# Last attention of a Flamingo-style block: per-head context scores in row tiles, one reduction for head 0's maximum, an early load of the exponential table, the residual part of the norm moved by one tile

## What is computed

```python
xn = layer_norm(x, g_x, b_x)          # here x is the context, 77 rows for each batch
ln = layer_norm(latents, g_l, b_l)    # the 1024 tokens
q = ln @ Wq;  k, v = split(concat([xn, ln], axis=1) @ Wkv)   # 16 heads of 64; 77 + 1024 keys
sim = (q * 64 ** -0.5) @ k.T          # per head
sim = where(full_mask, sim, max_neg)  # masks the 77 context keys alone
out = concat_heads(softmax(sim) @ v) @ Wout
return layer_norm(out, g_o, b_o)      # then x = x + tanh(g) * this
```

## Time and profile before

| | |
|---|---|
| median of three runs | 2142.96 us |
| the profiled execution | 2142.78 us, span 2140.9 us |
| busy over the span: PE, weight loads, DVE, ACT, GpSimd | 91%, 62%, 69%, 46%, 35% |
| stage 6, the 128 tiles | 1108.9 to about 2022 us |

### The profile page before, as it was taken

How to read it: one execution, slowest core, us unless ns; L and a number is a source line. 1 busy time by engine, 2 the same in 40 slices (tenths; PEclk the granted TensorE clock), 3 DMA queues, 4 the chain that set the end, 5 groups by cost and what they waited for, 6 DMA issues and landing times.

```text
span 2140.9 us, 32958 instructions
## 1 busy us (share of the span) xinstructions
PE 1954.5 (91%) x11541; PEld 1319.1 (62%) x11541; DVE 1485.3 (69%) x2932; ACT 975.0 (46%) x2083; POOL 752.8 (35%) x1146
## 2 busy tenths in 40 slices
PE   6997899688799979988879999999989999998899
PEld 3884899434499967874555555555655555554554
DVE  5774111475244458877868999999779999998655
ACT  5662334343012252227855555555445555554445
POOL 1002111002312200000026777777546777777400
PEclk9897899888999999998989999999999999999999
DMA  3703799304299860002002333333213333333201
GB/s 112 203 2 111 268 327 327 113 0 145 97 298 320 284 218 1 1 8 77 1 20 71 81 81 81 81 81 81 63 42 76 78 80 82 80 77 81 51 1 39
DMA packets 191184, 226.85 MB, mean 106 GB/s; under 512 B 28939, under 2 KB 167085, under 8 KB 191021
## 3 DMA queue, kind: packets, MB, share of 16 engines
q1 hardware_dynamic: 183725, 201.98, 32.2%
q0 software_dynamic: 7296, 22.78, 3.2%
HBM read 127.64 MB, written 29.91 MB: 74 GB/s over the span
## 4 chain that ended last, share of the span: by engine, by line
PE 45%; ACT 5%; DVE 4%; issue 1%; ACTq 0%; DVEq 0%
PE ps L641 41%; ACT w_odd L1791 3%; PE ps L1206 1%; PE ps L1207 1%; PE ps L1107 1%; DVE small L2520 1%; ACT L1791 0%; DVE w_odd L2529 0%; DVE small L2404 0%; ACT arena L1780 0%; PE ps L1116 0%; ACT xn_tok L1643 0%; DVE small L2516 0%; DVE arena L2477 0%; DVE lnst L2470 0%
## 5 line engine op out<-in xcount | busy, mean ns | idle before, releaser
L1902 POOL COPY arena<-w_odd 32x512 f32<-32x512 f32 x1024 | 623.7, 609 | 293.0 <-DVE w_odd L2529 240.7
L641 PE MATMUL ps<-arena,w_odd 128*128 128x128 f32 (+4 forms) x2352 | 441.9, 443 | 3.0 <-DVE arena L2196 1.2
L641 PE MATMUL ps<-arena 128*64 128x256 f32 (+4 forms) x3248 | 392.2, 370 | 8.3 <-DVE arena L2327 4.4
L2529 DVE STREAM_TRANSPOSE w_odd<-w_odd 128x1024 f32<-128x1024 f32 x256 | 315.8, 1244 | 25.4 <-ACT w_odd L1791 17.1
L641 PEld LDWEIGHTS ps<-arena 128*64 128x64 f32 (+4 forms) x3248 | 258.3, 155 | 120.1 <-issue 22.5
L1791 ACT ACTIVATE w_odd<-ps,small 128x1101 f32<-128x1101 f32 x256 | 301.0, 1178 | 53.2 <-DVE small L2521 52.2
L641 PEld LDWEIGHTS ps<-arena,w_odd 128*128 128x128 f32 (+3 forms) x2352 | 246.8, 188 | 107.3 <-issue 102.0
L2520 DVE TENSOR_REDUCE small<-ps 128x1 f32<-128x589 f32 (+1 forms) x256 | 253.6, 991 | 16.4 <-PE ps L641 16.4
L1776 ACT ACTIVATE arena<-ps 77x256 f32<-77x256 f32 x128 | 48.6, 379 | 321.8 <-PE ps L1207 321.7
L1886 POOL DMA_INDIRECT token_rows<-arena x62 | 59.9, 965 | 306.4 <-DVE arena L2217 306.4
L641 PE MATMUL ps<-xn_feat,w_even 128*128 128x512 f32 (+1 forms) x352 | 141.2, 533 | 6.1 <-DVE xn_feat L2101 1.9
(11 more groups left out here) (397 smaller groups left out, 3016.5 us busy)
## 6 DMA issues: line engine op xcount, KB each, us to landing
arena<-w_odd SPq DMA_DIRECT2D x1024, 64.0 KB
w_odd<-in_s_w SPq DMA_DIRECT2D x32, 1024.0 KB
w_odd<-in_s_wgu SPq DMA_DIRECT2D x30, 704.0 KB
w_even<-in_s_w SPq DMA_DIRECT2D x15, 1024.0 KB
arena<-expert_rows_in SPq DMA_DIRECT2D x62, 130.0 KB
w_odd<-in_s_wd SPq DMA_DIRECT2D x30, 256.0 KB
out_feat<-in_s_wgu SPq DMA_DIRECT2D x10, 704.0 KB, 4.2
expert_rows_in<-zero_row POOLq DMA_DIRECT2D x1, 5070.0 KB, 32.9
```

Source lines behind the costliest of these rows:

```text
L641: return pe.matmul(o, lhsT, rhs, start=start, stop=stop, **kw)
L1902: pool.tensor_copy(s6_d[u % 4][32 * j:32 * j + 32, :, 256 * i:256 * i + 256], s6_pm[u % 2][32 * i:32 * i + 32, :, 256 * j:256 * j + 256]). ...
L2529: dve.transpose(s6_pm[u % 2][:, h], s6_pm[u % 2][:, h]).then_inc(t6_done, 1)
```

## The change

1. PE computes the context scores of each head as a product of its own, contracting over that head's 64 partitions and 77 columns wide. The order is: context of head 0; first tokens of head 1; first tokens of head 0; a wait of PE for the completion of the context product of head 0; context of head 1; last tokens of head 0; last tokens of head 1. There are four increments of the semaphore a tile, before there were three.
2. `s6_kx` holds the 77 columns once; the memset on GpSimd, its semaphore and one of two ACT copies go.
3. DVE starts on the context scores when both are there, and takes head 0's maximum in one reduction of 1101 columns, behind the last token product. The reduction of 512 columns and one use of the two-operand minimum go.
4. Behind each square root of the output norm ACT takes an exponential of one column into a scratch cell.
5. `added(g)` runs one tile later, in the even tile ahead of `normed(g + 1)`, for g % 32 from 28 to 30; for g % 32 = 31 it stays where it was.

```diff
-        s6_kx = [cut(WE, 8704 + 154 * i, 2, C) for i in range(2)]
+        s6_kx = [cut(WE, 8704 + 154 * i, C) for i in range(2)]
...
-                    mm(s6_both, s6_q[n % 2][:, q0:q0 + P], s6_kx[n % 2]).then_inc(a6_s, 1)
-                    for i in range(2):
-                        for h in range(2):
-                            r = 64 * h
-                            last = mm(PS[:, 3 * h + i, :], s6_q[n % 2][r:r + 64, q0:q0 + P], s6_k[n % 2][r:r + 64, i * 512:(i + 1) * 512])
-                        last.then_inc(a6_s, 1)
+                    def tokens(h, i):
+                        r = 64 * h
+                        return mm(PS[:, 3 * h + i, :], s6_q[n % 2][r:r + 64, q0:q0 + P], s6_k[n % 2][r:r + 64, i * 512:(i + 1) * 512])
+
+                    def context(h):
+                        r = 64 * h
+                        return mm(s6_both[:, h], s6_q[n % 2][r:r + 64, q0:q0 + P], s6_kx[n % 2][r:r + 64])
+
+                    context(0).then_inc(a6_s, 1)
+                    tokens(1, 0)
+                    tokens(0, 0).then_inc(a6_s, 1)
+                    pe.wait_ge(a6_s, 4 * u + 1)
+                    context(1).then_inc(a6_s, 1)
+                    tokens(0, 1)
+                    tokens(1, 1).then_inc(a6_s, 1)
...
-                        if n < 2:
-                            act.wait_ge(z6_in, 1)
-                        act.activation(s6_kx[n % 2][0:64, 0], PS[0:64, bank, 2 * P:2 * P + C], ACT.Copy)
-                        last = act.activation(s6_kx[n % 2][64:P, 1], PS[64:P, bank, 2 * P:2 * P + C], ACT.Copy)
+                        last = act.activation(s6_kx[n % 2], PS[:, bank, 2 * P:2 * P + C], ACT.Copy)
...
                         act.activation(lnsd[:, t:t + 2], lnve[:, t:t + 2], ACT.Sqrt).then_inc(o6_sd, 1)
+                        act.activation(exp_cells[:, no:no + 1], zero[:, 0:1], ACT.Exp)
...
-                    pool.memset(WE[:, 8704:9012], 0.0).then_inc(z6_in, 1)
...
-                        dve.wait_ge(a6_s, 3 * u + 1)
+                        dve.wait_ge(a6_s, 4 * u + 3)
                         link(dve.tensor_tensor(s6_both, s6_both, s6_mk[:, u // 64].unsqueeze(1).broadcast_to([P, 2, C]), ALU.add))
                         dve.tensor_reduce(s6_cm[:, u % 2, 1:2], s6_both[:, 1], AX.X, ALU.max, negate=True)
-                        dve.wait_ge(a6_s, 3 * u + 2)
-                        dve.tensor_reduce(s6_cm[:, u % 2, 0:1], psf[:, 0:512], AX.X, ALU.max, negate=True)
-                        dve.wait_ge(a6_s, 3 * u + 3)
-                        for h in range(2):
-                            m = s6_nm[:, u % 2, h:h + 1]
-                            link(dve.tensor_reduce(m, s6_rest[h], AX.X, ALU.max, negate=True))
-                            dve.tensor_tensor(m, m, s6_cm[:, u % 2, h:h + 1], ALU.min).then_inc(a6_mx, 1)
+                        dve.wait_ge(a6_s, 4 * u + 4)
+                        dve.tensor_reduce(s6_nm[:, u % 2, 0:1], s6_sc[0], AX.X, ALU.max, negate=True).then_inc(a6_mx, 1)
+                        m = s6_nm[:, u % 2, 1:2]
+                        link(dve.tensor_reduce(m, psf[:, 3 * 512:3 * 512 + S], AX.X, ALU.max, negate=True))
+                        dve.tensor_tensor(m, m, s6_cm[:, u % 2, 1:2], ALU.min).then_inc(a6_mx, 1)
...
+                    if even and u >= 6 and 28 <= (u // 2 - 3) % 32 < 31:
+                        added(u // 2 - 3)
                     if even and u >= 4 and (u // 2 - 2) % 32 >= 28:
                         normed(u // 2 - 2)
-                    if not even and u >= 5 and ((u - 1) // 2 - 2) % 32 >= 28:
+                    if not even and u >= 5 and ((u - 1) // 2 - 2) % 32 == 31:
                         added((u - 1) // 2 - 2)
```

More of the change, by code:

```diff
@@ L113, in build @@
         vo_t = cut(WO, 0, 4, 8, D, rows=C)
-        ln_bias, sqrt_cell = cut(small, 320, NT), cut(small, 141, 1)
+        ln_bias, sqrt_cell, exp_cells = cut(small, 320, NT), cut(small, 141, 1), cut(small, 144, 8)
         s4_wk = cut(WE, 0, KD, H * DH)
@@ L1799, in stage6 @@
                         copied(act, ("o", g))
+                        no = 4 * (g // 32) + g % 4
                         act.activation(lnsd[:, t:t + 2], lnve[:, t:t + 2], ACT.Sqrt).then_inc(o6_sd, 1)
+                        act.activation(exp_cells[:, no:no + 1], zero[:, 0:1], ACT.Exp)
                     if u == 73:
```

## The result

| | before | after |
|---|---|---|
| median of six runs, same session | 2142.98 us | 2119.3 us (2117.94 to 2123.16) |
| ratio, 95% interval | | 0.9893 (0.988 to 0.9906) |
| the profiled execution, its span | 2142.78, 2140.9 us | 2120.45, 2118.7 us |

What follows compares the result with a forecast made beforehand. Two bounds in turn: PE's own work and the loop of scores, maxima, exponentials, next scores, its minimum stalled by GpSimd's copies. Regular tiles +5.0, the other changes -17.8, sum -12.8 from 2142.78: 2130 us, range 2100 to 2140.

Steps and rivals of the forecast that it cites:

- The gap case: Regular tiles: the minimum starts by 4.61, between two GpSimd copies; eight tiles 51.5 us, total 2106; chance 0.26.
- The term +5.0: Some 106 regular tiles: loop 6.66 us, eight tiles 53.3 against 52.92, so +5.0 us in all.
- now ACT is idle and needs 0.1, as ahead of the first: Regular tile: second exponential starts 0.1 us behind its maximum, at 5.34, giving next scores at 6.66.
- its own case: Whole kernel: the forecast of 2130 us with a spread of 2121 to 2137; chance 0.58.
- The added wait: PE's wait for head 0's context product: costs nothing under queued token passes, about half a microsecond without that cover.
- The case of strict order: Rival, PE in regular tiles: passes keep program order, last tokens end at 2.96, loop 7.33, total 2200; chance 0.05.
- The draining wait: Rival, PE's new wait: passes only when all issued before is done; loop about 7.2, total 2183; chance 0.06.
- Tiles 60 to 68: Early table load in odd tiles -5.6 us, later `added` -3.8 in tiles 62, 64, 66 and -0.7 in 60, 68.
- The end: From tile 120 on: -0.3 (120 to 124), -2.8 (125, 127), -1.4 (126), -3.5 (last projections), +0.3 us (useless load).
- The -0.3 of tiles 120 to 124: Tiles partly at the low clock, shorter scores against the loop's added 0.08; -0.3 us, an estimate.
- The load that has no use: Table load in tiles 128 and 130, which have no exponential: hidden but for about +0.3 us ahead of stage 7.
- the second wait: Behind the last scores PE waits 2.53 and 1.03 us for line 2510 behind `added`; -3.5 us for both.

Runs made afterwards that it cites:

- After_ts: Changed kernel with head 1's minimum taking its second value as a per-partition scalar (tensor_scalar); ratio 0.9855 to the kernel before, eight tiles 51.89 us against 52.72.
- three_waits: Changed kernel with ACT waiting for the same three semaphores ahead of both exponentials; ratio 0.9946 to the kernel before, eight tiles 53.38 us.
- bare_wait: Changed kernel with PE's wait directly behind head 0's context product, first tokens moved behind head 1's context; ratio 1.018 to the kernel before, eight tiles 56.43 us.
- best: After_ts without the scratch exponential in tiles 128 and 130, plus one behind tile 73's square root; 2096.76 us, ratio 0.9853 to the kernel before.
- Table_only: Kernel before with part 4 alone, the scratch exponential behind each square root; 2124.07 us, ratio 0.998.
- added_only: Kernel before with part 5 alone, `added` one tile later; 2123.04 us, ratio 0.9972.
- norm_only: Kernel before with parts 4 and 5 alone, scores and maxima as before; ratio 0.9926 to the kernel before.

## Why the prediction was right, and where it was off

**The regular tile, mechanism.** Each step up to the minimum came out within 0.02 us of the forecast (in brackets): last tokens done at 2.21 (2.21), the 1101 columns in 1.30 (1.29), maxima at 3.56 (3.54) and 5.24 (5.23), the minimum held by a copy in most tiles. After_ts shows that it is the copy. The gap case failed for the reason given: the minimum starts at 4.73, past the start of the sixth copy (4.62).

**The regular tile, size.** The term +5.0 measured -2.3, and this is 7.3 of the 9.4 us by which the sum was short. The step that failed is "now ACT is idle and needs 0.1, as ahead of the first". The second exponential starts 0.04 behind its maximum though ACT is idle, and the loop is 6.60 instead of 6.66: 8 x 6.60 = 52.8 instead of 53.3, and 106 x 0.06 = 6.4 us, most of the 7.3. The 0.1 ahead of the first exponential belongs to its three waits, not to idleness; three_waits gave the second exponential three waits and brought the forecast's number back.

**The range.** That the median lies in the range is in part luck. The prediction gave its own case 2121 to 2137, and 2119.3 lies below that; the range reached down to 2100 for the gap case, which did not come.

**The added wait** costs nothing under its cover (tokens end at the 2.21 of the sum without it) and 0.49 us without (bare_wait), as argued. What the uncovered wait does to a tile was expected too low, because PE's own need was left out of that expectation.

**PE's order.** The case of strict order (2200) is refuted. Both heads' first passes start 0.01 apart and the last tokens end at 2.21, not 2.96. The Trainium skill, "TensorE: Matmul & The Clock Gate", section "The mechanism", has matmuls start and end in program order; for products on different halves of the rows this trace disagrees. In each of the 128 tiles head 1's first token pass starts ahead of the second pass of head 0's context product (0.01 and 0.17 in the tile shown), which the program gives first. The draining wait (2183) is refuted by the same 2.21.

**Tiles 60 to 68.** Forecast -10.1, measured -10.65. Tiles 62, 64 and 66 gave -3.83 (-3.8 forecast), tiles 60 and 68 -0.70 (-0.7), and tiles 61 to 67 -6.1 (-5.6): the exponential starts 0.21 behind its maximum, not 0.3, which is most of the difference.

**The end.** Forecast -7.7, measured -9.8. The -0.3 of tiles 120 to 124 says little: these tiles take from 39.4 to 41.3 us in the traces (bare_wait apart), and 41.05 to 41.25 in the three kernels with the old scores and the norm's parts, against 40.79 before. The load that has no use costs 0.4 (0.3): the last feed-forward takes 93.05 us in the kernel before, 93.45 in the changed one and 93.13 in best, which leaves that load out. What was missing is the clock: only tile 126 was given a part of it, but the row of 3.75 us in the earlier trace rows is itself a slow one, and 1.8 us of it went when PE no longer idled ahead of it. Against that only half of the second wait went (1.03 to 0.53). Table_only and added_only show that this gain, about 4 us, came only with both parts.

**What stays open.** The start of tile 0 is 0.55 later in the changed kernel; nothing before it was changed but a memset and the ACT copy, and in the other twelve traces that start varies by 6 us, whatever the kernel, so this cannot be told from chance. Why the same idle time lowered the clock in tile 69 of two traces (norm_only, bare_wait) and not of others is not settled either.

## What to carry to other kernels

When an operation's duration comes in two values (159 and 600 ns here), look for whose instruction it ends with: a loop that passes through it has the length of that other engine's train, and work removed elsewhere in the loop gives nothing back until this is cut; here another form of the same operation did it. Before a start delay is carried from one place to another, compare what the two instructions wait for. Where either of two nearby idle times of PE goes with a lower granted clock (0.86 and 0.89 here, 1.00 with both gone), they should be priced together, not one by one.

## What the runs showed of the hardware

- A minimum of two operands of one element a partition, both in SBUF, lasted until GpSimd's running copy ended (159 to 608 ns; all 105 of over 250 ns ended 0.01 us behind a copy). The same minimum with the second operand as per-partition scalar took 211 to 215 ns beside the same copies.
- An exponential that waits for one semaphore started 0.04 us behind it, with ACT idle; with three semaphores, two of them long passed, 0.11 us.
- A wait of PE for its own product held it 0.49 us uncovered and nothing with a 512-column product of each head issued in between.
- Products on different halves of PE's rows did not start in program order: head 1's first token pass started at 0.01, the second pass of head 0's earlier product at 0.17, likewise in all 128 tiles.
- The table load of 1.28 us was followed by the next activation within 0.02 us (1527.69 + 1.28, then 1528.99).
